# Edge loop of a graph layer on one core: the leaky slope in two halves, with the additions around it reordered

## The chip, the cores and the metric

The kernel runs on one core of one Trainium2 chip. The metric is the device time of one execution in microseconds (us), as the median of several runs. Three runs of the kernel before gave 2620.51, 2626.28 and 2626.96 us, median 2626.28.

## The reference, cut to what matters

Two layers of a graph network over 6,250 nodes of 128 features and 100,000 edges. Only the first layer's edge part matters here:

```python
f = (e @ fc_w.T).reshape(-1, 4, 128)          # 4 heads
w = attn[rel]                                 # one of 100 relations per edge
feat = sum over heads of leaky_relu(w * f, negative_slope=0.2)
msg = h[src] + feat
agg = segment_sum(msg, dst)                   # the edges come sorted by dst
x = layernorm(x + agg)
```

The second layer (an attention over the same edges) and a second layer norm follow. The change does not touch them.

## The kernel before, in words

The 100,000 edges are padded to 196 groups (`G0`) of 512 edges, each group held as `TG` = 4 tiles `u` of 128 edges. One loop goes over the groups; it runs once here (196 operations of `y` are in the profile). Each engine has its own in-order program for the loop, written out by hand, and semaphores tie them together:

- **TensorE** (`group`, L932). For group g: `products` for u = 0 and 1 (L889; the matmul L896 makes f in the PSUM banks `FP[u // 2]`, L905 makes w in `WP[u % 2]`), then `aggregate(g - 2)` (L909: L915 and L917 sum messages by destination into the PSUM bank AP), then `products` for u = 2 and 3, then `compact(g)` (L928, sorting work for the second layer). `aggregate` waits for `x_added` at L910. Everything behind it in TensorE's program waits too.
- **ScalarE** (`step`, L695). Per group: `blocks` (L666), copy of w to SBUF for u = 0 (L659), `window_gap` (L676), copy u = 1, `relation` of the next group (L646, L651), copy u = 2, `window` (L685), copy u = 3, `compact` (L693).
- **VectorE** (`group`, L1258), the engine that the change touches. Per group g: `records` (L1205), `weigh_pair` 0 (L1224: z = f times w for u = 0 and 1), for the group before it `halve` (L1239: sums heads pairwise, `hs`) and `finish` (L1247: `msg`), then `weigh_pair` 1 (u = 2 and 3), `accumulate(g - 2)` (L1215: adds AP to 64 columns of `accT`), for the group before it `add_x` (L1255: adds the gathered x rows to three of four tiles of `msg`, signals `x_added`), and last `slope(g)` (L1231: y = max(0.2 z, z) over all four tiles, 2048 elements per partition).
- **GpSimd** (L534, L542). Four indirect gathers of x rows per group (L539), four groups ahead, released by `agg_done`, and one indirect scatter (L550). **SyncE** issues the loads of e and of the relation numbers (L459, L463).

So the messages of group g - 1 are finished in VectorE's turn for group g, and TensorE sums them in its turn for group g + 1, between the two halves of that group's products. `weigh_pair` 1 of a group waits for `f_done` (L896) and `w_copied` (L659, u = 3).

Of the kernel before, what the change touches and what calls it, by code (L numbers as in the profile page):

```python
# [5 lines left out]
ALU = mybir.AluOpType  # L6
# [50 lines left out]
SLOPE0, SLOPE1, EPS = 0.2, 0.01, 1e-5  # L57
# [15 lines left out]
def build(nc, x, x_t, e, src_pg, dst_pg, dst_g, rel_g, fcT, attn, WT, Wn, b, a1, a1b, a2, a2b, out):  # L73
    with ExitStack() as ctx:
        def sb(name, shape, dt=F32):
            return ctx.enter_context(nc.sbuf_tensor(name, shape, dt))

        def sem(name):
            return ctx.enter_context(nc.semaphore(name))
# [98 lines left out]
        z = sb("z", [P, 2, 2, D4])  # L178
        y = sb("y", [P, 2, 2, D4])
# [153 lines left out]
        z_done = sem("z_done")  # L333
        y_done = sem("y_done")
# [702 lines left out]
        def _(dve):  # L1037
            v = nc.vector
# [162 lines left out]
            def records(g, k, lead):  # L1201

                if not (lead and k < 2):
                    dve.wait_ge(r_done, g - 1)
                v.tensor_tensor(joh[:, k % 2, :, :], iota_row[:, 0:J].rearrange("p (o w) -> p o w", o=1)  # L1205
                                .to_broadcast([P, TG, J]),
                                rank[:, bass.ds(g * TG, TG)].rearrange("p (u o) -> p u o", o=1)
                                .to_broadcast([P, TG, J]), ALU.is_equal).then_inc(joh_ready, 1)

            def accumulate(g, k, lead):  # L1210
                r = dve.value_load(base_rep[0:1, bass.ds(g, 1)], min_val=0, max_val=NP)  # L1211
                dve.wait_ge(agg_done, g + 1)
                if not (lead and k == 0):
                    dve.wait_ge(acc_done, g)
                v.tensor_tensor(accT[:, bass.ds(r, W)], accT[:, bass.ds(r, W)], AP_[:, 0:W],  # L1215
                                ALU.add).then_inc(acc_done, 1)

            def weigh_pair(g, k, lead, h):

                dve.wait_ge(f_done, 2 * g + h + 1)  # L1220
                dve.wait_ge(w_copied, TG * g + 2 * h + 2)
                if not (lead and k == 0):
                    dve.wait_ge(y_done, g)
                v.tensor_tensor(z[:, h, :, :], FP[h][:, :, :], w_sb[:, h, :, :], ALU.mult).then_inc(z_done, 1)  # L1224

            def slope(g, k, lead):

                dve.wait_ge(z_done, 2 * g + 2)
                if not (lead and k == 0):
                    dve.wait_ge(hs_done, g)  # L1230
                v.scalar_tensor_tensor(y[:, :, :, :], z[:, :, :, :], SLOPE0, z[:, :, :, :], ALU.mult,  # L1231
                                       ALU.max).then_inc(y_done, 1)

            def halve(g, k, lead):

                dve.wait_ge(y_done, g + 1)
                if not (lead and k == 0):
                    dve.wait_ge(msg_ready, g)
                v.tensor_tensor(hs[:, :, :], y_all[:, :, 0:D4 // 2], y_all[:, :, D4 // 2:D4],  # L1239
                                ALU.add).then_inc(hs_done, 1)  # L1240

            def finish(g, k, lead):

                dve.wait_ge(hs_done, g + 1)
                if not (lead and k < 2):
                    dve.wait_ge(agg_done, g - 1)
                v.tensor_tensor(msg[:, k % 2, :, :], hs[:, :, 0:P], hs[:, :, P:2 * P],  # L1247
                                ALU.add).then_inc(msg_ready, 1)

            def add_x(g, k, lead):  # L1250

                dve.wait_ge(msg_ready, g + 1)
                dve.wait_ge(xg_in[k], PASS_IN * p + 16 * TG + (g - k) * 16)
                dve.sem_inc(dve_turn, 1)
                v.tensor_tensor(msg[:, k % 2, 0:X_DVE, :], msg[:, k % 2, 0:X_DVE, :], xg[:, k, 0:X_DVE, 0:P],  # L1255
                                ALU.add).then_inc(x_added, 1)

            def group(g, k, lead):  # L1258
                prev = None if lead and k == 0 else (g - 1, (k - 1) % SLOTS, lead)
                records(g, k, lead)  # L1260
                weigh_pair(g, k, lead, 0)
                if prev:
                    halve(*prev)
                    finish(*prev)
                weigh_pair(g, k, lead, 1)
                if not (lead and k < 2):
                    accumulate(g - 2, (k - 2) % SLOTS, lead)
                if prev:
                    add_x(*prev)
                slope(g, k, lead)  # L1270

            with dve.Fori(0, pass_count(dve)) as p:
                for k in range(SLOTS):
                    group(k, k, True)
                for g in range(SLOTS, G0):
                    group(g, g % SLOTS, False)
                halve(G0 - 1, SLOTS - 1, False)
                finish(G0 - 1, SLOTS - 1, False)
                add_x(G0 - 1, SLOTS - 1, False)
                accumulate(G0 - 2, SLOTS - 2, False)  # L1280

                dve.wait_ge(gap_made, G0)
                v.tensor_scalar(dloc[:, :], dloc[:, :], float(W), None, ALU.subtract).then_inc(win_step, 1)
                dve.wait_ge(joh_ready, G0)
                v.tensor_scalar(rank[:, :], rank[:, :], float(J), None, ALU.add).then_inc(win_step, 1)
                v.tensor_scalar(spot[:, :], spot[:, :], float(J), None, ALU.subtract).then_inc(win_step, 1)
                v.tensor_scalar(left[:, :], left[:, :], float(J), None, ALU.add).then_inc(win_step, 1)
                dve.wait_ge(win_step, 7 * p + 4)
                v.scalar_tensor_tensor(spot_m[:, :], left[:, :], 0.0, spot[:, :], ALU.is_gt,
                                       ALU.mult).then_inc(win_step, 1)  # L1290
                accumulate(G0 - 1, SLOTS - 1, False)
                dve.wait_ge(acc_done, G0)
                v.tensor_scalar(base_rep, base_rep, W, NP, ALU.add, ALU.min).then_inc(win_step, 1)
                dve.wait_ge(win_step, 7 * p + 6)
                for k in range(SLOTS):
                    dve.wait_ge(sc_in[k], PASS_SC * (p + 1))
                    dve.sem_inc(dve_turn, 1)
                v.tensor_scalar(spot_i[:, :], spot_m[:, :], trash[:, 0:1], None, ALU.add).then_inc(win_step, 1)
                dve.wait_ge(win_step, 7 * p + 7)
                meet(dve, p)  # L1300
# [235 lines left out]
            for j in range(TAIL):  # L1536
                k = j % S1
# [82 lines left out]
```

## Time and profile before

| | |
|---|---|
| span of the profiled execution | 2618.1 us |
| runs | 2620.51, 2626.28, 2626.96 us |
| median less span of the profile | 8.2 us |
| edge loop in the profile | about 82 to 1492 us |
| engines busy over the span | TensorE 82%, VectorE 86%, ScalarE 66%, GpSimd 73% |

The profiled execution has a span and no separate run time of its own. The span is the time from its first to its last recorded instruction; the runs lie 2.4 to 8.9 us above it.

How to read the rows: a line such as `1004.51 0.55 DVE L1255 TENSOR_TENSOR room<-room 128x384` is an instruction of VectorE (DVE) that started 1004.51 us into the span, took 0.55 us, is at line 1255, and writes and reads a tile of the memory block `room` (`msg` and the gathered rows lie in `room`). PE is TensorE's matmul, PEld its weight load, ACT ScalarE, POOL GpSimd. `[0.23 <-DVE room L1255]` says that the engine was idle for 0.23 us before the instruction and that L1255 on VectorE ended this. An instruction of VectorE can start a little before the one in front of it has ended, so what an instruction costs is the distance between starts, not its own duration.

### The profile page before, as it was taken

The page shows a single profiled execution, that of the slowest core. Times are in us where ns is not written, and L with a number is a line of the kernel's source. Part 1 is how long each engine was busy: PE and PEld are TensorE (multiplying, and loading weights), DVE is VectorE, ACT ScalarE, POOL GpSimd, SP SyncE. Part 2 cuts the span into 40 slices and gives each one's busy share as a digit, 9 for nine tenths or more (in the row PEclk, how much of TensorE's full clock was granted, in tenths as well). Part 3 has the DMA queues.
Part 4 walks back from the last instruction along what each step waited for, and adds up shares of the span by engine and source line. Part 5 has one row for each costly group of instructions (what it writes and reads, how often), then busy time and mean ns, then how long its engine had stood idle before and what let it go on. Part 6 is the DMA issues. An engine that isn't in the chain of part 4 may idle for free.

```text
span 2618.1 us, 44445 instructions
## 1 busy us (share of the span) xinstructions
PE 2159.8 (82%) x11261; PEld 1538.3 (59%) x11261; DVE 2255.1 (86%) x5754; ACT 1740.7 (66%) x4973; POOL 1919.3 (73%) x1845
## 2 busy tenths in 40 slices
PE   6999999999999999999999846665666666666664
PEld 3566666666666666666666535565656565556554
DVE  9999999999999999999999976666666666677887
ACT  5888888888888888888888644444444444444446
POOL 2487777777777777777777647777777777777773
PEclk8999999999999999999999877777677767777776
DMA  4233333333333333333333233333333333333343
GB/s 133 78 100 104 104 104 103 106 103 102 103 103 105 104 105 105 103 103 102 103 104 104 65 95 81 80 80 80 81 81 80 81 81 82 79 81 79 80 80 80
DMA packets 156600, 244.04 MB, mean 93 GB/s; under 512 B 40836, under 2 KB 84398, under 8 KB 156226
## 3 DMA queue, kind: packets, MB, share of 16 engines
q1 hardware_dynamic: 97730, 132.55, 17.9%
q0 software_dynamic: 58624, 108.72, 17.5%
q8 instruction: 92, 1.51, 0.2%
q14 instruction: 154, 1.26, 0.2%
HBM read 231.99 MB, written 9.12 MB: 92 GB/s over the span
## 4 chain that ended last, share of the span: by engine, by line
DVE 36%; issue 25%; POOL 18%; PE 7%; DMA 6%; DVEq 5%; ACT 1%; POOLq 0%; SPq 0%; ACTq 0%
POOL room L583 17%; DVE y L1231 17%; DVE hs L1239 9%; DMA room<-h_rows,y 5%; DVEq L1211 4%; DVE room L1255 4%; PE FP L986 3%; DVE accT L1215 2%; PE FP L1007 2%; PE AP L1007 1%; DVE z L1224 1%; DMA room<-h_rows,idx 1%; DVE joh L1205 1%; POOL room L591 1%; DVE room L1247 1%
## 5 line engine op out<-in xcount | busy, mean ns | idle before, releaser
L539 POOL DMA_INDIRECT room<-in_x,pk x784 | 920.7, 1174 | 262.5 <-issue 251.0
L583 POOL DMA_INDIRECT room<-h_rows,y x756 | 714.7, 945 | 235.2 <-issue 216.0
L896 PE MATMUL FP<-fc_sb,room 128*128 128x512 f32 x1568 | 832.3, 612 | 2.2 <-issue 2.2
L905 PE MATMUL WP<-at_p,rel_oh 100*128 100x512 f32 x1568 | 803.5, 594 | 0.0
L986 PE MATMUL FP<-ident,room 128*128 128x128 f32 x1664 | 342.7, 370 | 385.9 <-DMA room<-h_rows,y 351.7
L659 ACT ACTIVATE w_sb<-WP 128x512 f32<-128x512 f32 x784 | 464.1, 592 | 225.0 <-PE WP L905 219.7
L986 PEld LDWEIGHTS FP<-ident,room 128*128 128x128 f32 x1664 | 291.0, 263 | 433.3 <-DMA room<-h_rows,y 387.1
L757 ACT ACTIVATE accT<-accT,neg_big 128x512 f32<-128x512 bf16 x208 | 150.0, 722 | 559.6 <-DVE accT L1377 559.6
L905 PEld LDWEIGHTS WP<-at_p,rel_oh 100*128 100x128 f32 x1568 | 297.8, 190 | 376.5 <-issue 376.5
L1224 DVE TENSOR_TENSOR z<-FP,w_sb 128x1024 f32<-128x1024 f32 x392 | 478.6, 1221 | 1.6 <-ACT w_sb L659 1.0
L1231 DVE SCALAR_TENSOR_TENSOR y<-z 128x2048 f32<-128x2048 f32 x196 | 452.4, 2308 | 0.0
L896 PEld LDWEIGHTS FP<-fc_sb,room 128*128 128x128 f32 x1568 | 266.3, 189 | 43.1 <-issue 2.6
L776 ACT ACTIVATE room<-room,pr 128x129 f32<-128x129 f32 x832 | 266.6, 392 | 6.8
L550 POOL DMA_INDIRECT sorted_edges<-runs,spot_i x196 | 190.4, 972 | 90.6 <-issue 60.5
L666 ACT ACTIVATE boh<-arena,rank_pay 128x52 f32<-128x52 bf16 x784 | 239.8, 378 | 0.0
L1239 DVE TENSOR_TENSOR hs<-y 128x1024 f32<-128x1024 f32 x196 | 238.3, 1216 | 0.0
L915 PEld LDWEIGHTS AP<-doh,room 128*128 128x128 f32 x1568 | 190.6, 192 | 54.1 <-DVE room L1255 54.1
L915 PE MATMUL AP<-doh,room 128*128 128x64 f32 x1568 | 211.9, 278 | 6.8 <-DVE accT L1215 3.9
L676 ACT ACTIVATE dot<-iota_row,dloc 128x64 bf16<-128x64 f32 x784 | 206.3, 336 | 0.0
L1387 DVE SCALAR_TENSOR_TENSOR arena<-arena,decay,AP 128x129 f32 x104 | 36.2, 348 | 175.5 <-PE AP L1007 158.9
L1420 DVE CUSTOM_DVE_ANT_0 hs<-accT,FP 128x512 f32<-128x512 f32 x208 | 142.0, 683 | 17.8 <-PE FP L986 11.8
L1387 DVE SCALAR_TENSOR_TENSOR arena<-arena,decay,FP 128x129 f32 x104 | 36.0, 347 | 124.8 <-PE FP L1007 108.2
(246 smaller groups left out, 3181.6 us busy)
## 6 DMA issues: line engine op xcount, KB each, us to landing
room<-in_e SPq DMA_DIRECT2D x196, 256.0 KB, 2.7
rel_sb<-in_rel_g SPq DMA_DIRECT2D x196, 200.0 KB
z<-sorted_sources SPq DMA_DIRECT2D x208, 128.0 KB, 3.0
room<-in_x,pk POOLq DMA_INDIRECT x784
room<-h_rows,y POOLq DMA_INDIRECT x756
sorted_edges<-runs,spot_i POOLq DMA_INDIRECT x196, 2.0
accT<-in_x_t SPq DMA_DIRECT2D x1, 3125.0 KB, 11.2
h_rows<-arena SPq DMA_DIRECT2D x13, 227.5 KB, 2.8
```

The lines of the kernel that those rows point to most:

```text
L539: pool.indirect_dma_start(xg[:, k, u, 0:P], None, x[:, :], bass.IndirectOffsetOnAxis(ap=pk[:, g, u:u + 1], axis=0)).then_inc(xg_in[k], 16)
L583: pool.indirect_dma_start(hg[k][:, u, :], None, h_dram[:, :], bass.IndirectOffsetOnAxis(ap=sd[:, g * TG + u:g * TG + u + 1], axis=0)).then ...
L659: nc.scalar.activation(w_sb[:, u // 2, u % 2, :], WP[u % 2][:, :], ACT.Copy).then_inc(w_copied, 1)
L666: ins = nc.scalar.activation(boh[:, k % 2, u, :], onehot[:, :, bass.ds(g * TG + u, 1)].rearrange("p b o -> p (b o)"), ACT.Identity, bias=0 ...
L776: nc.scalar.activation(hg[k][:, u, 0:P + 1], hg[k][:, u, 0:P + 1], ACT.Identity, bias=0.0, scale=pr[:, k % 2, u:u + 1]).then_inc(h_scaled, 1)
L896: mm = pe.matmul(FP[u // 2][:, u % 2, :], e_sb[:, k, u, :], fc_sb[:, :], start=True, stop=True)
L905: mm = pe.matmul(WP[u % 2][:, :], rel_oh[:, k % 2, u * P:(u + 1) * P], at_p[:, j, :], start=(j == 0), stop=(j == 1))
L915: pe.matmul(AP_[:, 0:W], msg[:, k % 2, u, :], doh[:, k % 2, u, :], start=(u == 0), stop=False)
L986: mm = pe.matmul(rows_of(k)[:, u * P:(u + 1) * P], hg[k][:, u, P + 1:P + 2].to_broadcast([P, P]), ident[:, :], start=True, stop=True)
L1224: v.tensor_tensor(z[:, h, :, :], FP[h][:, :, :], w_sb[:, h, :, :], ALU.mult).then_inc(z_done, 1)
L1231: v.scalar_tensor_tensor(y[:, :, :, :], z[:, :, :, :], SLOPE0, z[:, :, :, :], ALU.mult, ALU.max).then_inc(y_done, 1)
L1239: v.tensor_tensor(hs[:, :, :], y_all[:, :, 0:D4 // 2], y_all[:, :, D4 // 2:D4], ALU.add).then_inc(hs_done, 1)
```

## The change

`slope` becomes `slope_pair`, which makes y for one half (u = 0 and 1, or u = 2 and 3) of 1024 elements per partition. The two halves stand on either side of `add_x`, and `accumulate(g - 2)` moves from behind `weigh_pair` 1 to between `halve` and `finish`. The counts of `y_done` double, and the waits on it are rewritten to the new counts.

```diff
@@ -1220,20 +1220,20 @@
                 dve.wait_ge(f_done, 2 * g + h + 1)
                 dve.wait_ge(w_copied, TG * g + 2 * h + 2)
                 if not (lead and k == 0):
-                    dve.wait_ge(y_done, g)
+                    dve.wait_ge(y_done, 2 * g - 1 + h)
                 v.tensor_tensor(z[:, h, :, :], FP[h][:, :, :], w_sb[:, h, :, :], ALU.mult).then_inc(z_done, 1)
 
-            def slope(g, k, lead):
-
-                dve.wait_ge(z_done, 2 * g + 2)
+            def slope_pair(g, k, lead, h):
+
+                dve.wait_ge(z_done, 2 * g + h + 1)
                 if not (lead and k == 0):
                     dve.wait_ge(hs_done, g)
-                v.scalar_tensor_tensor(y[:, :, :, :], z[:, :, :, :], SLOPE0, z[:, :, :, :], ALU.mult,
+                v.scalar_tensor_tensor(y[:, h, :, :], z[:, h, :, :], SLOPE0, z[:, h, :, :], ALU.mult,
                                        ALU.max).then_inc(y_done, 1)
 
             def halve(g, k, lead):
 
-                dve.wait_ge(y_done, g + 1)
+                dve.wait_ge(y_done, 2 * g + 2)
                 if not (lead and k == 0):
                     dve.wait_ge(msg_ready, g)
                 v.tensor_tensor(hs[:, :, :], y_all[:, :, 0:D4 // 2], y_all[:, :, D4 // 2:D4],
@@ -1261,13 +1261,15 @@
                 weigh_pair(g, k, lead, 0)
                 if prev:
                     halve(*prev)
-                    finish(*prev)
-                weigh_pair(g, k, lead, 1)
                 if not (lead and k < 2):
                     accumulate(g - 2, (k - 2) % SLOTS, lead)
                 if prev:
+                    finish(*prev)
+                weigh_pair(g, k, lead, 1)
+                slope_pair(g, k, lead, 0)
+                if prev:
                     add_x(*prev)
-                slope(g, k, lead)
+                slope_pair(g, k, lead, 1)
```

## Rows read from the trace of the kernel before

**Rows 1.** The page: span, and the busy time of each engine.
```profile
span 2618.1 us, 44445 instructions
PE 2159.8 (82%) x11261; PEld 1538.3 (59%) x11261; DVE 2255.1 (86%) x5754; ACT 1740.7 (66%) x4973; POOL 1919.3 (73%) x1845
```

**Rows 2.** Busy time by stretch, the edge loop; busy us per engine, clock, DMA share.
```profile
core 0: us, PE busy (x) PEld busy (x) DVE busy (x) ACT busy (x) POOL busy (x), PEclk, DMA share, GB/s
...
155.00:1478.00 1323.00, 1322.69 (x6273) 820.18 (x6271) 1316.14 (x1475) 1107.49 (x2951) 1042.95 (x920) 1.00 0.35 103
```

**Rows 3.** Who waited for whom, 500 to 1400 us: longest waits, and VectorE's only one.
```profile
ACT w_sb L659 <- PE WP L905: 138.6, 346, 0.9
...
PEld AP L915 <- DVE room L1255: 30.4, 126, 0.6
...
DVE z L1224 <- issue: 0.3, 1, 0.3
```

**Rows 4.** Timeline of VectorE, one group from L1205 to L1231.
```profile
1000.03 0.28 DVE L1205 TENSOR_TENSOR joh<-iota_row,rank_pay 128x128 f32<-128x128 f32 x1
1000.24 1.23 DVE L1224 TENSOR_TENSOR z<-FP,w_sb 128x1024 f32<-128x1024 f32 x1
1001.38 1.22 DVE L1239 TENSOR_TENSOR hs<-y 128x1024 f32<-128x1024 f32 x1
1002.63 0.69 DVE L1247 TENSOR_TENSOR room<-hs 128x512 f32<-128x512 f32 x1
1003.24 1.22 DVE L1224 TENSOR_TENSOR z<-FP,w_sb 128x1024 f32<-128x1024 f32 x1
1004.38 0.21 DVE L1215 TENSOR_TENSOR accT<-accT,AP 128x64 f32 x1
1004.51 0.55 DVE L1255 TENSOR_TENSOR room<-room 128x384 f32<-128x384 f32 x1
1004.98 2.31 DVE L1231 SCALAR_TENSOR_TENSOR y<-z 128x2048 f32<-128x2048 f32 x1
```

**Rows 5.** Timeline of VectorE, the next group: L1205, L1224 twice.
```profile
1007.21 0.28 DVE L1205 TENSOR_TENSOR joh<-iota_row,rank_pay 128x128 f32<-128x128 f32 x1
1007.41 1.23 DVE L1224 TENSOR_TENSOR z<-FP,w_sb 128x1024 f32<-128x1024 f32 x1
...
1010.41 1.22 DVE L1224 TENSOR_TENSOR z<-FP,w_sb 128x1024 f32<-128x1024 f32 x1
```

**Rows 6.** Timeline of VectorE, the first and the last of 196 L1231.
```profile
86.50 2.29 DVE L1231 SCALAR_TENSOR_TENSOR y<-z 128x2048 f32<-128x2048 f32 x1
...
1485.81 2.28 DVE L1231 SCALAR_TENSOR_TENSOR y<-z 128x2048 f32<-128x2048 f32 x1
```

**Rows 7.** Timeline of TensorE and ScalarE from the aggregation to copies of u = 3.
```profile
1005.11 0.97 PEld L915 LDWEIGHTS AP<-doh,room 128*128 128x128 f32 x8 [0.23 <-DVE room L1255]
...
1006.28 1.08 PE L896 MATMUL FP<-fc_sb,room 128*128 128x512 f32 x2
...
1008.12 1.02 PE L905 MATMUL WP<-at_p,rel_oh 100*128 100x512 f32 x2
...
1009.18 0.60 ACT L659 ACTIVATE w_sb<-WP 128x512 f32<-128x512 f32 x1 [0.42 <-PE WP L905]
```

**Rows 8.** Timeline of the loop's start: L1255 of group 0 to the copy behind it.
```profile
93.06 0.55 DVE L1255 TENSOR_TENSOR room<-room 128x384 f32<-128x384 f32 x1
...
97.72 0.60 ACT L659 ACTIVATE w_sb<-WP 128x512 f32<-128x512 f32 x1 [0.41 <-PE WP L905]
```

**Rows 9.** Timeline of the loop's start: a copy and the L1224 that waited for it.
```profile
84.56 0.59 ACT L659 ACTIVATE w_sb<-WP 128x512 f32<-128x512 f32 x1
...
85.25 1.23 DVE L1224 TENSOR_TENSOR z<-FP,w_sb 128x1024 f32<-128x1024 f32 x1 [1.02 <-ACT w_sb L659]
```

**Rows 10.** Timeline of ScalarE: copy of u = 1 that L1224 at 1007.41 needs.
```profile
1005.48 0.58 ACT L659 ACTIVATE w_sb<-WP 128x512 f32<-128x512 f32 x1
```

**Rows 11.** Busy time by stretch: TensorE's clock where it is partly idle.
```profile
78.00:82.00 4.00, 3.04 (x9) 1.81 (x10) 3.58 (x5) 1.44 (x5) 0.00 (x0) 1.00 0.07 26
...
1485.00:1490.00 5.00, 1.61 (x10) 1.42 (x10) 4.93 (x6) 0.00 (x0) 1.99 (x1) 0.68 0.02 3
```

## The prediction

> **What bounds the kernel now.** The page comes first: VectorE has the largest busy share, TensorE the next [rows 1]. That is an average over two layers, so the second view is the busy time by stretch. In the edge loop VectorE is busy for 1316 of 1323 us and TensorE for all of it, at a granted clock of 1.00 [rows 2]. Two full engines need a third view, who waits for whom: VectorE waits once in 900 us, for 0.3 us; TensorE's weight load of the aggregation waits 126 times for L1255, 0.24 us each; ScalarE waits for TensorE [rows 3]. So **VectorE sets the pace**, and TensorE, which looks as busy, is held back a little by it once per group.
>
> The fourth view is the timeline of one group [rows 4, 5]. The distances between starts are: L1205 0.21, z 1.14, hs 1.25, msg 0.61, z 1.14, accT 0.13, add_x 0.47, y 2.23, together 7.18. From the first to the last y there are 195 periods in 1399.31 us, 7.176 each [rows 6]. Nearly every instruction starts 0.08 us before its forerunner ends. The exception is `finish` behind `halve`: it reads what `halve` just wrote, and starts 0.03 after its end.
>
> The same timeline holds the **loop between engines**, which isn't the bound today. add_x ends at 1004.51 + 0.55 = 1005.06. The aggregation's first weight load follows at 1005.11, the products of u = 2 at 1006.28, the last w product at 1008.12, and ScalarE's copy of u = 3 runs from 1009.18 to 1009.78 [rows 7]. From the end of add_x to the end of that copy are 4.72 us. The z of that half starts at 1010.41 [rows 5], so its input was ready 0.63 us early. That 0.63 is all the room in the loop.
>
> **The change, part by part.**
>
> *Accumulate moved.* `finish` must still wait for `halve`, but accumulate now stands between. Before, hs and accT cost 1.25 + 0.13; after, hs takes its unhindered 1.14 (as z does) and accT 0.13, and `finish` starts just after hs has ended. Gain on VectorE 0.11 per group, at least 0.08, at most 0.11. Its own input isn't late: the aggregation that it needs ends some 1.4 us after add_x, and accumulate comes over 3 us after add_x even when moved.
>
> The Trainium skill, page "VectorE: DVE Perf Modes", section "The DRAIN you can't avoid", says that a semaphore between two VectorE operations costs nothing extra. The trace differs: 1.25 against 1.14. By that rule this part would gain nothing, and VectorE's own period would be 7.22 instead of the 7.11 below.
>
> *y in two.* y of 2048 elements takes 2.31, hs of 1024 takes 1.22 [rows 4]; 1024 elements more cost 1.09. A half thus costs 2.23 - 1.09 = 1.14 between starts, two of them 2.28, 0.05 more than one. Bounds: nothing below 0, and at most the whole difference of durations, 2 x 1.22 - 2.31 = 0.13. I take 0.05, since all of VectorE's large operations overlap their forerunner. The second half ends, as before, with L1205 and a z between it and `halve`, so no wait appears there.
>
> *The waits on y_done.* z of half 0 waits for the half 0 of the group before, z of half 1 for its half 1. Both lie far behind on the same in-order engine: nothing. slope_pair 0 waits for the z of half 0, also long done: nothing.
>
> Sum for VectorE alone: 7.17 - 0.11 + 0.05 = **7.11**, that is 0.06 less per group, 12 us in all.
>
> *add_x comes later: the part that decides.* Before, add_x ends 1.14 + 0.13 + 0.55 = 1.82 us after the start of the second z. After, it ends 1.14 (z) + 1.14 (slope_pair 0) + 0.55 = 2.83 after it: 1.01 later. TensorE's program has the aggregation ahead of the products of u = 2 and 3, so these, ScalarE's copies of them and the next group's second z are all later by as much. There was room for 0.63, less 0.06 that VectorE's shorter period takes. The loop closes:
>
> - end of add_x to end of the copy of u = 3: 4.72 [rows 4, 7]. The first group with an aggregation gives 97.72 + 0.60 - 93.61 = 4.71 [rows 8].
> - end of the copy to the z that waits for it: 85.25 - 85.15 = 0.10 [rows 9].
> - z to slope_pair 0 to end of add_x: 2.83.
>
> Together **7.65 us per group** against 7.176. VectorE needs only 7.11 and so waits 0.54 us before the second z of each group. The loop acts from group 2 on, 194 groups: 194 x 0.474 = 92 us. The gains of the other parts are inside that wait and bring nothing.
>
> Bounds of the 7.65: the array still streams the last w product when the aggregation comes today, and it will be empty then, so the 4.72 could shrink to 4.60 if the aggregation starts quicker. The handover from the copy could be 0.03, as between TensorE and ScalarE (1008.12 + 1.02 to 1009.18), or 0.12. slope_pair 0 costs 1.14 to 1.22. Each alone moves the period by 0.1 or less; together 7.52 to 7.73 is plausible, 67 to 108 us.
>
> *What else hangs on it.* The first z of a group needs the copy of u = 1, which ends at 1006.06 against 1007.41 [rows 10, 5], 1.35 early. ScalarE reaches it about 4.05 us after the start of the copy of u = 3, and by that it will still be some 0.7 us early. GpSimd gathers four groups ahead behind the aggregation, SyncE loads e behind the products; nothing is moved on their queues, each gets a longer period, and their covers are whole groups: nothing. The second layer is untouched.
>
> The sum is made against the profiled execution: 2618.1 + 92 = 2710 of span, and with the 8.2 us by which the median lies above the span, 2718.
>
> **The rivals.**
>
> *VectorE stays the bound and the kernel gets faster.* This needs the path from add_x to the end of the copy, handover included, to take no more than 7.11 - 2.83 = 4.28 us instead of 4.82. For it: TensorE looks full today, and some of its 4.72 could be old work that an idle array would not have. Against it: the path is two products, ten short matmuls and a copy behind the wait, and it took 4.71 and 4.72 in two states. It gives 2614, with the full 0.13 for the split 2630. Chance 0.07. By the skill's rule on semaphores, above, this case would give 7.22 and 2635 instead.
>
> *The loop closes, but with less excess.* TensorE overlaps more after an idle stretch, so the path loses 0.2 to 0.3 us. The period would be 7.35 to 7.45: 2660 to 2680. Nothing in the trace shows it. Chance 0.05.
>
> *TensorE's clock falls.* TensorE would idle about half a microsecond per group. Where it was busy for 1.61 of 5 us, the clock was 0.68; where it was busy for 3.04 of 4, it was 1.00 [rows 11]. Here it stays busy for over 90%. If the clock fell to half in one group of ten, the four microseconds of TensorE on the path would double there: 19 x 4 = 76 us more, 2794. Chance 0.04. The skill's page "TensorE: Matmul & The Clock Gate", section "Part 1: The HAM clock gate (the "warmup" mystery)", says that an idle array falls to 1.2 GHz; the 0.68 agrees.
>
> *The change doesn't do what it says.* y is in two only if the two instructions run as written; the diff leaves no other reading. No chance of its own.
>
> **How the numbers follow.** The forecast has 0.84, with its own range 2690 to 2735. A difference of 0.3%, 8 us, is about what a measurement of this kernel can tell from no change. Faster by more than that is only the better part of the first rival: 0.04. Within 0.3%: its rest, 0.03. Slower: forecast, smaller excess and clock, 0.93. The range for 8 times in 10 goes a little beyond the forecast's own, for the bounds of the unknown terms: 2682 to 2738.
>
> **What would show it right or wrong.** In the waits of the changed kernel, L1224 should wait for ScalarE's copy L659 once per group, some 0.5 us, about 100 us in all, and the aggregation's weight load should wait some 0.7 us for L1255 instead of 0.24. VectorE's busy share in the loop should fall to about 93%, and its starts should repeat every 7.65 us. From the end of add_x to the end of the copy of u = 3 should be 4.6 to 4.75. `finish` should start at or right behind the end of hs with accT between, and each half of y should take 1.2 us. The prediction is wrong if VectorE shows no wait before the second z (then the path is shorter than I read it), if the wait stands before the first z (then ScalarE's order decides), or if the clock in the loop is under 1.00.

## The result and the profile after

The changed kernel takes 2710.78 us (median of 4 runs, 2709.55 to 2711.36) against 2624.86 (2620.51 to 2626.96): ratio 1.0329, 95% interval 1.0315 to 1.0344. It is slower by 86 us; forecast were 92, and 2718 us. By the spans, 2709.1 against 2618.1 [rows 1], it is 91.0.

The page of the changed kernel: span, busy times, and three groups of its fifth part (busy us, mean ns, idle before and its releaser).
```profile
span 2709.1 us, 44836 instructions
PE 2200.7 (81%) x11261; PEld 1542.3 (57%) x11261; DVE 2259.2 (83%) x5950; ACT 1741.6 (64%) x4973; POOL 2000.1 (74%) x1845
...
L1224 DVE TENSOR_TENSOR z<-FP,w_sb 128x1024 f32<-128x1024 f32 x392 | 478.7, 1221 | 93.2 <-ACT w_sb L659 69.3
...
L1231 DVE SCALAR_TENSOR_TENSOR y<-z 128x1024 f32<-128x1024 f32 x392 | 477.1, 1217 | 0.0
L915 PEld LDWEIGHTS AP<-doh,room 128*128 128x128 f32 x1568 | 190.5, 192 | 142.5 <-DVE room L1255 142.5
```

VectorE has only 4 us more of busy time. The other 87 of the 91 us are idle time, and nearly all of it stands before z: 93.2 us in all (some 2 us of this were there before). The weight load of the aggregation waits 142.5 us for add_x.

Who waited for whom, 500 to 1400 us, and the busy times of the edge loop; these answer to [rows 3, 2].
```profile
PEld AP L915 <- DVE room L1255: 82.1, 118, 0.7
...
DVE z L1224 <- ACT w_sb L659: 42.0, 90, 0.5
...
DVE z L1224 <- issue: 12.9, 28, 0.5
```
```profile
155.00:1478.00 1323.00, 1277.16 (x5897) 771.59 (x5896) 1242.48 (x1561) 1043.14 (x2778) 1057.89 (x867) 1.00 0.36 98
```

VectorE's share in the loop fell from 99.5% to 93.9%. Once per group it waits for the last copy; the 28 waits put down to "issue" are the same wait at the same place. The aggregation waits 0.70 us instead of 0.24. The clock stays at 1.00.

Timeline of VectorE, from the second z of one group to that of the next; it answers to [rows 4, 5].
```profile
1001.39 1.22 DVE L1224 TENSOR_TENSOR z<-FP,w_sb 128x1024 f32<-128x1024 f32 x1 [0.48 <-ACT w_sb L659]
1002.53 1.22 DVE L1231 SCALAR_TENSOR_TENSOR y<-z 128x1024 f32<-128x1024 f32 x1
1003.66 0.55 DVE L1255 TENSOR_TENSOR room<-room 128x384 f32<-128x384 f32 x1
1004.13 1.22 DVE L1231 SCALAR_TENSOR_TENSOR y<-z 128x1024 f32<-128x1024 f32 x1
1005.26 0.28 DVE L1205 TENSOR_TENSOR joh<-iota_row,rank_pay 128x128 f32<-128x128 f32 x1
1005.47 1.22 DVE L1224 TENSOR_TENSOR z<-FP,w_sb 128x1024 f32<-128x1024 f32 x1
1006.60 1.22 DVE L1239 TENSOR_TENSOR hs<-y 128x1024 f32<-128x1024 f32 x1
1007.74 0.21 DVE L1215 TENSOR_TENSOR accT<-accT,AP 128x64 f32 x1
1007.87 0.68 DVE L1247 TENSOR_TENSOR room<-hs 128x512 f32<-128x512 f32 x1
1009.01 1.23 DVE L1224 TENSOR_TENSOR z<-FP,w_sb 128x1024 f32<-128x1024 f32 x1 [0.46 <-issue]
```

Between them, the aggregation's weight load and the copy of u = 3; they answer to [rows 7].
```profile
1004.26 0.97 PEld L915 LDWEIGHTS AP<-doh,room 128*128 128x128 f32 x8 [0.70 <-DVE room L1255]
...
1008.32 0.60 ACT L659 ACTIVATE w_sb<-WP 128x512 f32<-128x512 f32 x1 [0.41 <-PE WP L905]
```

The loop can be read off. add_x ends at 1003.66 + 0.55 = 1004.21, the copy at 1008.92: 4.71. The next z starts 0.09 later. From z to the end of add_x are 1.14 + 1.13 + 0.55 = 2.82. Together **7.62**, which is the distance of the two z.

### The profile page after: what moved, and what is told of

The parts are those of the page before. It is cut to its first block, busy times and chain, and to the rows that moved or that the text cites. A ratio compares the mean times of both kernels' runs of the same rounds, so it can differ in the third digit from the quotient of the medians.

```text
span 2709.1 us, 44836 instructions
## 1 busy us (share of the span) xinstructions
PE 2200.7 (81%) x11261; PEld 1542.3 (57%) x11261; DVE 2259.2 (83%) x5950; ACT 1741.6 (64%) x4973; POOL 2000.1 (74%) x1845
## 4 chain that ended last, share of the span: by engine, by line
PE 36%; issue 18%; DVE 18%; POOL 17%; DMA 6%; ACT 4%; DVEq 1%; POOLq 0%; SPq 0%; ACTq 0%
POOL room L583 17%; PE FP L896 13%; DVE y L1231 9%; PE AP L915 8%; PE WP L905 7%; DMA room<-h_rows,y 5%; ACT w_sb L659 4%; DVE room L1255 3%; PE FP L986 3%; PE AP L1007 2%; PE AP L917 2%; PE FP L1007 1%; DVE z L1224 1%; DMA room<-h_rows,idx 0%; DVE arena L1076 0%
## 5 line engine op out<-in xcount | busy, mean ns | idle before, releaser
L539 POOL DMA_INDIRECT room<-in_x,pk x784 | 1000.7, 1276 | 264.8 <-issue 248.6
L1224 DVE TENSOR_TENSOR z<-FP,w_sb 128x1024 f32<-128x1024 f32 x392 | 478.7, 1221 | 93.2 <-ACT w_sb L659 69.3
L1231 DVE SCALAR_TENSOR_TENSOR y<-z 128x1024 f32<-128x1024 f32 x392 | 477.1, 1217 | 0.0
L915 PEld LDWEIGHTS AP<-doh,room 128*128 128x128 f32 x1568 | 190.5, 192 | 142.5 <-DVE room L1255 142.5
L915 PE MATMUL AP<-doh,room 128*128 128x64 f32 x1568 | 217.4, 282 | 58.3 <-DVE room L1255 55.2
L1379 DVE TENSOR_TENSOR accT<-z,WP 128x512 bf16<-128x512 bf16 x208 | 141.5, 681 | 0.7 <-DVE room L1372 0.7
```

Source lines behind the costliest of these rows:

```text
L539: pool.indirect_dma_start(xg[:, k, u, 0:P], None, x[:, :], bass.IndirectOffsetOnAxis(ap=pk[:, g, u:u + 1], axis=0)).then_inc(xg_in[k], 16)
L915: pe.matmul(AP_[:, 0:W], msg[:, k % 2, u, :], doh[:, k % 2, u, :], start=(u == 0), stop=False)
L1231: v.scalar_tensor_tensor(y[:, h, :, :], z[:, h, :, :], SLOPE0, z[:, h, :, :], ALU.mult, ALU.max).then_inc(y_done, 1)
```

## The experiments

Two theories of the changed kernel stood at first. The loop: the period is the larger of VectorE's own sum and of 4.80 us plus the time from the second z to the end of add_x. The rival: the split itself costs, by its instruction and its waits. A third was that TensorE has no slack of its own.

### The loop, made longer

e3 puts accumulate back between the second z and the first half of y. This and the other differences below are cut to the lines that matter:

```diff
                 if prev:
                     halve(*prev)
-                if not (lead and k < 2):
-                    accumulate(g - 2, (k - 2) % SLOTS, lead)
-                if prev:
                     finish(*prev)
                 weigh_pair(g, k, lead, 1)
+                if not (lead and k < 2):
+                    accumulate(g - 2, (k - 2) % SLOTS, lead)
                 slope_pair(g, k, lead, 0)
```

> The changed kernel with accumulate back behind the second z, so inside the stretch from z to add_x. Loop: 0.13 to 0.14 more between z and add_x, period 7.76, 26 us more than the changed kernel, 2737. If VectorE's idle 0.48 per group is only slack, an operation of 0.13 and a handover of 0.11 vanish in it: 2711.

It took 2738.43 us (before beside it 2621.97; ratio 1.0442, 1.0426 to 1.0458), 27.7 more than the changed kernel. VectorE idles half a microsecond per group, and an operation of 0.13 us in the wrong place still costs its full length, 194 times (27.7 / 194 = 0.14). Its wait sits where it sat before:
```profile
1001.91 1.23 DVE L1224 TENSOR_TENSOR z<-FP,w_sb 128x1024 f32<-128x1024 f32 x1 [0.49 <-ACT w_sb L659]
1003.05 0.21 DVE L1215 TENSOR_TENSOR accT<-accT,AP 128x64 f32 x1
```

e4 leaves the kernel before as it was, but for add_x, which goes behind the whole y:

```diff
+                slope(g, k, lead)
                 if prev:
                     add_x(*prev)
-                slope(g, k, lead)
```

> The kernel before with add_x behind the whole of y; no instruction is added or split. Loop: 4.80 + 1.14 + 0.13 + 2.23 + 0.55 = 8.85 per group, 1.67 more than before, 194 x 1.67 = 325, so 2950. 'The split itself costs' expects 2625, since nothing is split.

It took 3190.35 us. The direction was right, the size wasn't: 568 us were lost, not 325. Its busy times by stretch (busy us per engine, then the clock), the wait of its aggregation from 500 to 1500 us, and two of its second z point at the reason.
```profile
500.00:700.00 200.00, 171.28 (x674) 100.26 (x673) 142.27 (x159) 119.25 (x319) 111.90 (x100) 0.87 0.26 74
...
1000.00:1010.00 10.00, 8.54 (x35) 5.26 (x33) 6.71 (x9) 5.59 (x16) 4.47 (x5) 0.83 0.26 68
1010.00:1020.00 10.00, 8.15 (x37) 4.64 (x35) 8.36 (x9) 7.17 (x22) 7.22 (x5) 1.00 0.28 75
```
```profile
PEld AP L915 <- DVE room L1255: 185.2, 98, 1.9
```
```profile
1008.16 1.22 DVE L1224 TENSOR_TENSOR z<-FP,w_sb 128x1024 f32<-128x1024 f32 x1 [3.25 <-ACT w_sb L659]
...
1016.98 1.23 DVE L1224 TENSOR_TENSOR z<-FP,w_sb 128x1024 f32<-128x1024 f32 x1 [1.61 <-ACT w_sb L659]
```
In the stretch where the clock was 1.00, the period is 8.82, as expected (8.85). TensorE now waits 1.9 us per group for add_x, its clock is granted at 0.83 in other stretches, and there a group takes longer: y to y 10.47 us (998.96 to 1009.43). The matmul of f takes 732 ns on average over this kernel, against 612 in the kernel before. So the rival with the falling clock is real, at a wait of 1.9 us, not at the 0.70 of the changed kernel. That the clock makes up all of the missing 243 us is read from the trace; no run tests it alone.

### The loop opened by VectorE: two misses

e1 moves accumulate alone, the rest as before:

```diff
                 if prev:
                     halve(*prev)
-                    finish(*prev)
-                weigh_pair(g, k, lead, 1)
                 if not (lead and k < 2):
                     accumulate(g - 2, (k - 2) % SLOTS, lead)
                 if prev:
+                    finish(*prev)
+                weigh_pair(g, k, lead, 1)
+                if prev:
                     add_x(*prev)
                 slope(g, k, lead)
```

> Accumulate moved alone, y in one operation, add_x right behind the second z. Theory of the loop (period = the larger of VectorE's own sum and of 4.80 us from the end of add_x to the next second z plus the time from that z to the end of add_x): the loop needs 4.80 + 1.14 + 0.55 = 6.49, VectorE 7.06, so 7.06 per group, about 22 us less than before, 2603. Rival 'TensorE has no slack of its own' (in the changed kernel its group would take 7.19 without the 0.43 by which the aggregation starts late): the period stays near 7.17 and the time near 2625, with waits for ScalarE's copy or none on VectorE.

e2 is the changed kernel with add_x ahead of both halves of y:

```diff
                 weigh_pair(g, k, lead, 1)
-                slope_pair(g, k, lead, 0)
                 if prev:
                     add_x(*prev)
+                slope_pair(g, k, lead, 0)
                 slope_pair(g, k, lead, 1)
```

> The changed kernel with add_x ahead of both halves of y: the split and the move of accumulate stay. Loop: 4.80 + 1.14 + 0.55 = 6.49, VectorE 7.10, so about 14 us less than before, 2611. 'TensorE has no slack': 7.17, near 2625. Rival 'the split itself costs, by its extra instruction or its waits': the time stays near the changed kernel's 2711.

Both missed by far. e1 took **2857.37** us (ratio 1.0894, 1.0879 to 1.0909), e2 2754.84 (1.0506, 1.0492 to 1.0520). All theories so far fall for these two. The waits of e1, 500 to 1500 us:
```profile
ACT runs L693 <- DMA sorted_edges<-runs,spot_i: 293.7, 110, 4.3
...
DVE z L1224 <- ACT w_sb L659: 107.6, 105, 3.3
...
DVE room L1255 <- DMA room<-in_x,pk: 41.3, 47, 2.2
```
ScalarE waits for the scatter, VectorE for the gathers: GpSimd is late. It was never late before, and nothing was changed on it. So its instructions were read one by one, first in the kernel before.
```profile
1004.96 0.98 POOL L539 DMA_INDIRECT room<-in_x,pk  x1 [0.30 <-issue]
1006.25 1.86 POOL L539 DMA_INDIRECT room<-in_x,pk  x1 [0.30 <-issue]
1008.41 0.94 POOL L539 DMA_INDIRECT room<-in_x,pk  x1 [0.30 <-issue]
1009.66 0.95 POOL L539 DMA_INDIRECT room<-in_x,pk  x1 [0.30 <-issue]
1010.91 0.93 POOL L550 DMA_INDIRECT sorted_edges<-runs,spot_i  x1 [0.30 <-issue]
1012.14 0.98 POOL L539 DMA_INDIRECT room<-in_x,pk  x1 [0.30 <-issue]
```
Then e1, with VectorE's y.
```profile
1013.82 2.28 DVE L1231 SCALAR_TENSOR_TENSOR y<-z 128x2048 f32<-128x2048 f32 x1
...
1014.04 2.88 POOL L539 DMA_INDIRECT room<-in_x,pk  x1 [0.30 <-issue]
```
An instruction of GpSimd takes 0.93 to 0.98 us, unless it starts while VectorE works on an operation with two inputs from SBUF; then it ends 0.82 us behind that operation, where this is later. In the kernel before, y runs from 1004.98 to 1007.29 [rows 4], and 1007.29 + 0.82 is 8.11, where the instruction of 1.86 ends. In e1, 1013.82 + 2.28 + 0.82 = 1016.92 = 1014.04 + 2.88. That is read from durations; no view lists it as a wait. The thirteen traces bear it out between 90 and 1480 us: 3,291 gathers and scatters of over 1.02 us end 0.77 to 0.87 us behind such an operation, and the 3,846 that start inside a z alone take 0.91 to 1.00. In the changed kernel two are held per group, one by each half of y (1002.53 + 1.22 + 0.82 = 1004.57, and 1004.13 + 1.22 + 0.82 = 1006.17):
```profile
1002.61 1.95 POOL L539 DMA_INDIRECT room<-in_x,pk  x1 [0.31 <-issue]
1004.87 1.30 POOL L539 DMA_INDIRECT room<-in_x,pk  x1 [0.30 <-issue]
```
**GpSimd had no slack in the kernel before.** From the end of y, a held instruction and its gap take 1.12, three free ones 1.25, 1.25 and 1.23: the next starts 4.85 us after the end of y, and must start before the next y does. In the kernel before it starts 0.02 us before it (1004.96 and 1004.98). With y of 2.31 that asks for 7.16 us from y to y; VectorE gives 7.17. In e1 it gives 7.03 where nothing holds it up, the instruction falls into y, and GpSimd loses over a microsecond per group. In e2 the halves of y stand together, and another operation, hs, holds an instruction too, to over 1.1 us: in 102 of its 113 groups from 500 to 1400 us, against 1 of 125 in the kernel before and none of 118 in the changed kernel. One of e2's, held by an hs from 1007.48 to 1008.69:
```profile
1007.52 2.02 POOL L539 DMA_INDIRECT room<-in_x,pk  x1 [0.30 <-issue]
```
That this is what e2 loses by was read from the trace, not tested.

The Trainium skill, page "SBUF — State Buffer", section "Terms", speaks of a port pair that VectorE and GpSimd arbitrate for, held for the whole instruction, the loser fully blocked. The trace agrees for GpSimd, and not for VectorE: a y that starts 0.02 us behind the start of a gather takes 2.31 us, and the last y, with no gather started just ahead of it, 2.28 [rows 6]. That the hold comes from this port is the page's account; the runs show the durations.

### GpSimd's phase, tested

e6 takes L917 out of e1's TensorE program, so that the x rows of the fourth tile are not summed. e6b also leaves out their gather (the counts that VectorE waits for follow it):

```diff
-                for u in range(TG):
+                for u in range(X_DVE):
                     pool.indirect_dma_start(xg[:, k, u, 0:P], ...
```

> The kernel with accumulate moved alone, and the x rows of the fourth tile are not summed (L917 left out), GpSimd's work unchanged. TensorE is relieved of 0.22 us per group. If GpSimd's gathers are what made that kernel 2857, the time stays within 1% of it. If TensorE had no slack, the time falls well below.

> As e6, and the x rows of the fourth tile are not gathered either: GpSimd has four instructions per group instead of five, VectorE and TensorE as in e6. Theory of GpSimd: four fit into 7.06, so VectorE sets the pace: about 2603, no wait for the scatter on ScalarE, none for the gathers on VectorE. If anything else than GpSimd holds the moved accumulate back, near 2857.

e6 took 2855.72 us, e6b **2593.65** (before 2621.92; ratio 0.9893, 0.9877 to 0.9908). TensorE's 0.22 us per group are worth nothing, one instruction of GpSimd 262 us. In e6b VectorE sets the pace (y to y is 7.03 throughout), and up to about 270 us GpSimd waits for TensorE in each group:
```profile
104.25 1.08 POOL L539 DMA_INDIRECT room<-in_x,pk  x1 [2.20 <-PE AP L915]
```
Later such waits are rare (4 of more than 0.35 us from 500 to 1400 us): the scatter starts behind y's start and is held for 2.93 us instead, and four instructions still fit into 7.03. The time is 9 us better than the expected 2603; 6 of these are that VectorE's real sum was 7.03, not 7.06 (y at 88.15, 95.18 and 102.20).

e7 and e8 keep all of e1, and each adds one of these operations, which do nothing useful, behind the second z. It is to slow VectorE down.

```diff
                 weigh_pair(g, k, lead, 1)
+                v.memset(cen[:, 0:64], 0.0)                                     # e7
+                v.tensor_tensor(cen[:, 0:64], iota_row[:, 0:64],                # e8
+                                neg_big[:, 0:1].to_broadcast([P, 64]), ALU.mult)
                 if prev:
                     add_x(*prev)
```

> The kernel with accumulate moved alone, plus a memset of 64 elements of an unused tile behind the second z, some 0.12 us of VectorE that do nothing. VectorE's sum is 7.18 again, y starts as late against the y before as in the kernel before, and GpSimd's fifth instruction again starts ahead of y: near 2626, that is 230 us less than without the filler. If it is the place of accumulate that hurts, the filler adds up to 24 us: 2857 to 2880.

e7 took 2860.82 us, as e1. It tells nothing for or against: the memset didn't fill.
```profile
101.74 0.11 DVE L1269 MEMSET cen<- 128x64 f32 x1
101.77 0.50 DVE L1255 TENSOR_TENSOR room<-room 128x384 f32<-128x384 f32 x1
102.18 2.28 DVE L1231 SCALAR_TENSOR_TENSOR y<-z 128x2048 f32<-128x2048 f32 x1
```
With the memset, add_x starts 1.21 us after z (100.56) instead of 1.14, but y only 0.41 after add_x instead of 0.47, and y comes 7.04 us after the y before (95.14). So a filler was needed that takes time.

> As the kernel with accumulate moved and a filler, but with a filler that takes VectorE's time: a tensor_tensor of 64 elements of an unused tile behind the second z, accumulate's own size, 0.13 between starts (the memset added 0.03 and shortened add_x's 0.47 to 0.41, so that VectorE's sum stayed at 7.04). VectorE's sum is 7.17 to 7.19 again. Theory of GpSimd, with y to y at 7.16 or more so that four undisturbed instructions and one held one fit: 2620 to 2632. If the place of accumulate hurts, or any period of this order is too short: 2855 to 2885.

e8 took **2620.54** us (before 2621.59; ratio 0.9996, 0.9986 to 1.0005). A useless operation of 0.13 us made e1 faster by 237 us, with accumulate left in its new place. So neither that place nor TensorE's work made e1 slow. Its timeline is that of the kernel before: a gather slips in 0.03 us ahead of y, the next is held.
```profile
1006.47 0.98 POOL L539 DMA_INDIRECT room<-in_x,pk  x1 [0.30 <-issue]
1006.50 2.30 DVE L1231 SCALAR_TENSOR_TENSOR y<-z 128x2048 f32<-128x2048 f32 x1
...
1007.76 1.85 POOL L539 DMA_INDIRECT room<-in_x,pk  x1 [0.30 <-issue]
```

### The loop opened by TensorE

e5 keeps the changed VectorE program and moves one call of TensorE's:

```diff
+                products(g, k, lead, 2)
                 if not (lead and k < 2):
                     aggregate(g - 2, (k - 2) % SLOTS, lead)
-                products(g, k, lead, 2)
                 products(g, k, lead, 3)
```

> The changed kernel, VectorE's program untouched, with TensorE's aggregation behind the products of u = 2 instead of ahead of them. Theory of the loop: one product of 1.32 us less lies between add_x and the next second z, the loop needs 7.62 - 1.33 = 6.29, and VectorE's own 7.11 becomes the period, if GpSimd keeps up: 2612. Theory of GpSimd (a gather or scatter that starts while VectorE works on an operation with two inputs from SBUF ends 0.82 us behind that operation instead of 0.94 after its start; its five instructions then take over a period or fit into it, by their phase): worked out over this order, GpSimd's group also takes 7.11. If the split itself or its waits cost, the time stays at 2711; if GpSimd falls behind as in the run with add_x first, 2750, with ScalarE's L693 waiting for the scatter.

It took **2606.09** us (before 2621.92; ratio 0.9941, 0.9927 to 0.9954): 105 us less than the changed kernel, and faster than the kernel before. Its loop and one of its waits, 500 to 1400 us:
```profile
155.00:1460.00 1305.00, 1305.00 (x6243) 831.96 (x6242) 1304.69 (x1654) 1098.72 (x2940) 1022.48 (x918) 1.00 0.38 104
```
```profile
POOL room L539 <- PE AP L917: 37.8, 124, 0.3
```
VectorE waits for nobody. GpSimd keeps up, but with hardly any room. TensorE now releases one of its gathers in nearly every group (the line above), yet the gap before it is the 0.30 us that stands before all of them, so no time goes by it; up to about 240 us one gap per group was 0.41 to 0.45, so some 0.13 us was to spare there. Each half of y holds one instruction, and for less than a whole y can:
```profile
1004.18 1.43 POOL L539 DMA_INDIRECT room<-in_x,pk  x1 [0.30 <-DMA sorted_edges<-runs,spot_i]
...
1005.92 1.30 POOL L539 DMA_INDIRECT room<-in_x,pk  x1 [0.30 <-issue]
...
1007.52 0.95 POOL L539 DMA_INDIRECT room<-in_x,pk  x1 [0.30 <-PE AP L917]
```

e9 puts TensorE's new order into the kernel before, e10 into e1, with the same edit as above.

> The kernel before with TensorE's aggregation behind the products of u = 2, nothing else. The loop had 0.6 us of room already and VectorE's 7.17 stays the period: 2618 to 2626, the time before. If TensorE's order is by itself worth what the run with both edits gained, 2606.

> Accumulate moved alone, y whole, with TensorE's new order. Theory of GpSimd: the order of TensorE doesn't touch what holds GpSimd, one y of 2.3 us per 7.06: within 1% of 2857, ScalarE waiting for the scatter. If the run with both edits was fast only because the loop was opened, this one is as fast or faster: 2600.

e9 took 2621.53 us (before 2621.59; ratio 1.0000, 0.9990 to 1.0010), e10 2841.53 (1.0826, 1.0798 to 1.0854). The order alone is worth nothing where the loop has room, and with y whole it doesn't save e1. The gain of e5 needs y in halves around add_x (without it e10, 2842) and the opened loop (without it the changed kernel, 2711). What the moved accumulate adds to it was not tested alone.

## Why the prediction was right

- **The bound and the room of the loop.** Right for what decides. The path from add_x to the copy was put at 4.72, measured 4.71; the handover at 0.10, measured 0.09; z to the end of add_x at 2.83, measured 2.82. The period was put at 7.65 and is 7.62. e3 and e5 show the cause from both sides: 0.13 us more in the loop cost 27.7 us; 1.33 us less took it off the critical path and gave back 105, down to VectorE's own sum.
- **VectorE's own sum.** Put at 7.11. e5 shows it: from the second half of y in group 1 to that of the last group are (1474.48 - 96.15) / 194 = 7.105. TensorE, with all its work, follows in that time, so the theory that it has no slack falls too. The split costs little: the halves stand 1.13 us from what follows, 2.26 together against 2.23.
- **Accumulate as a cover.** Right: hs, accT and msg start 1.14 and 0.13 apart. With y whole the move saved 0.15 per group (e1's 7.03), not the 0.11 that was its upper bound. Some 0.03 of it is y itself, which takes 2.28 instead of 2.31 where no gather starts just ahead of it.
- **The wait.** Forecast 0.54 us before the second z, measured 0.46 to 0.48, at the place that was named. The aggregation's wait was put at 0.7 and is 0.70.
- **The clock.** Stayed 1.00. e4 shows what it costs when it falls.
- **The sum.** 92 us of span expected, 91.0 measured. Of these, (1576.58 - 96.42) / 194 = 7.63 per group, from the second half of y in group 1 to that of the last group, gives 194 x 0.454 = 88. So the loop was put 4 us too high, and that the spans agree to 1 us is in part luck: the first z comes at 84.43 instead of 83.01, and what follows the loop takes 1.3 us more. The late start isn't the work of the change: the first z is at 84.12 in e9, where VectorE's program is untouched, and at 82.98 in e4. The median was put 7 too high, 6 of them by the step that added 8.2 us to the span: a run of the changed kernel with a span of 2709.1 took 2710.89, so 1.8 lie around the span. The median of three runs before was high too; over 19 later ones it is 2621.59.
- **GpSimd: the step that failed**, though the forecast didn't hang on it. "Their covers are whole groups: nothing" was wrong. Its program is four groups ahead by its semaphores, but not in time: without one wait shown, it took exactly as long as VectorE. In the changed kernel the period of 7.62 leaves it enough time, so the error stayed hidden.
- **The first rival** said 2614 for the changed VectorE program without the loop. e5 is just that, by a change on TensorE, and took 2606. So its price was sound; what it lacked was a path of 4.28 us. That GpSimd can follow was luck, and neither the rival nor the forecast had asked: e2, with nearly the same sum for VectorE and add_x first, took 2755. Of the orders tried with GpSimd's full work, only e5's has a period near 7.1 that it can follow.

## What to carry to other kernels

Before an operation that signals another engine is moved, follow the signal round until it comes back to the same engine, and add up the whole circle: if it is longer than the engine's own sum, it is the period, and free time elsewhere doesn't help. Where the circle can't be shortened on the one engine, look for a piece of work on the other that can go ahead of the wait. An engine that shows no wait and has the same period as the bound is not idle in between: compare the durations of its single instructions, for a longer one may be a wait that no view lists.

## What the runs showed of the hardware that was not expected

- An indirect DMA instruction of GpSimd that starts while VectorE works on an operation with two SBUF inputs ends 0.82 us (0.77 to 0.87 over all traces) after that operation, instead of 0.93 to 0.98 us after its own start. z, which reads PSUM and SBUF, doesn't hold it: in the kernel before, the gather at 1008.41 and the scatter at 1010.91 start inside a z [rows 5] and take 0.94 and 0.93.
- So two engines can lock in phase. With 7.17 us from y to y all goes well (the kernel before, e8, e9); with the 7.03 that VectorE could give, the same five instructions need over 8: e1 lost 235 us by saving 0.15 us per group.
- A memset of 64 elements between two large operations cost 0.01 us in all: add_x started 0.07 later, and y 0.06 sooner after add_x. A tensor_tensor of the same size cost 0.13.
- A wait of 0.70 us per 7.6 left TensorE's clock at 1.00; with a wait of 1.9 us per group (98 groups in 1000 us) it was 0.87 on average, and 0.83 in some stretches.
